# Second feed-forward matrix interleaved by tile and row half, both normalisations of a tile end to end, neighbour matrix split in two pieces among the roots

## The reference

```python
h1 = _layer_norm(x + attn_out, g1, be1)
ff = jax.nn.relu(h1 @ W1 + b1) @ W2 + b2
return _layer_norm(h1 + ff, g2, be2)          # added to x: "x1"
# next layer
h = jnp.maximum(_layernorm(x, axis=-1), 0.0)
alpha = x @ wc
beta = x @ wn                                  # x here is h
gamma = segment_sum(beta[dst], src) / counts[:, None]
x = x + alpha + gamma + bias
```

## Time and profile before

| what | us |
|---|---|
| median of 3 runs | 494.54 (494.07 to 494.81) |
| the profiled execution, as timed | 493.78 |
| its span in the profile | 491.9 |
| TensorE busy | 454.6 (92%) |
| VectorE busy | 309.4 (63%) |
| ScalarE busy | 192.4 (39%) |
| POOL busy | 164.3 (33%) |

### The profile page before, as it was taken

How to read it: one execution, slowest core, us unless ns; L and a number is a source line. 1 busy time by engine, 2 the same in 40 slices (tenths; PEclk the granted TensorE clock), 3 DMA queues, 4 the chain that set the end, 5 groups by cost and what they waited for, 6 DMA issues and landing times.

```text
span 491.9 us, 5957 instructions
## 1 busy us (share of the span) xinstructions
PE 454.6 (92%) x2107; PEld 333.7 (68%) x2107; DVE 309.4 (63%) x580; ACT 192.4 (39%) x265; POOL 164.3 (33%) x107
## 2 busy tenths in 40 slices
PE   3999997688869899889899999999999999999996
PEld 2456543334446778768678888888888888888865
DVE  5999845999975995877696223813361336142865
ACT  5878716546120531152351235222522342236240
POOL 3000141112242984539150433434342444145200
PEclk9999999999979999989998999999999999999999
DMA  8760000000030125202220023202321222220002
GB/s 267 205 225 1 1 1 23 0 1 0 1 107 0 52 94 198 85 1 107 88 83 4 0 98 139 95 12 87 120 88 71 87 107 85 87 85 1 0 1 85
DMA packets 22474, 34.34 MB, mean 70 GB/s; under 512 B 5680, under 2 KB 5936, under 8 KB 22448
## 3 DMA queue, kind: packets, MB, share of 16 engines
q1 hardware_dynamic: 22160, 33.85, 20.2%
q10 hardware_dynamic: 288, 0.13, 0.1%
HBM read 32.93 MB, written 1.05 MB: 69 GB/s over the span
## 4 chain that ended last, share of the span: by engine, by line
PE 70%; DVE 17%; POOL 5%; issue 3%; ACT 3%; DMA 1%; SPq 0%; POOLq 0%; DVEq 0%
PE ps L1177 15%; PE ps L1179 15%; PE ps L1178 15%; PE ps L1246 6%; PE ps L1239 4%; PE ps L1206 3%; PE ps L1205 3%; DVE rsum L894 3%; PE ps L1232 3%; DVE e_sb L375 2%; DVE stats L721 2%; POOL x_sb L479 1%; POOL w_lo L455 1%; DMA x_sb<-in_x 1%; DVE half_sum L891 1%
## 5 line engine op out<-in xcount | busy, mean ns | idle before, releaser
L454 POOL TENSOR_TENSOR w_lo<-w_stage,w_hi 128x1024 fp32r<-128x1024 f32 x22 | 52.7, 2394 | 137.7 <-ACT w_hi L530 137.7
L530 ACT ACTIVATE w_hi<-w_stage 128x2048 fp32r<-128x2048 f32 x23 | 44.0, 1911 | 73.0 <-PE ps L1179 73.0
L455 POOL TENSOR_TENSOR w_lo<-w_stage,w_hi 128x1024 fp32r<-128x1024 f32 x22 | 57.3, 2606 | 0.0
L1177 PE MATMUL ps<-w_hi,hid_hi 128*128 128x512 f32 x128 | 49.8, 389 | 0.0
L1178 PE MATMUL ps<-w_lo,hid_hi 128*128 128x512 f32 x128 | 49.8, 389 | 0.0
L1179 PE MATMUL ps<-w_hi,hid_lo 128*128 128x512 f32 x128 | 49.8, 389 | 0.0
L1086 DVE TENSOR_SCALAR tmp<-ps,bl 128x512 f32<-128x512 f32 x16 | 12.0, 751 | 52.1 <-ACT hid_hi L672 52.1
L1177 PE MATMUL ps<-T_hi,w_hi 128*128 128x512 f32 (+1 forms) x112 | 41.7, 372 | 1.8 <-DVE T_lo L751 1.4
L1178 PE MATMUL ps<-T_lo,w_hi 128*128 128x512 f32 (+1 forms) x112 | 40.7, 364 | 0.0
L1179 PE MATMUL ps<-T_hi,w_lo 128*128 128x512 f32 (+1 forms) x112 | 40.7, 363 | 0.0
L792 DVE TENSOR_SCALAR one_src<-iota_n,edge_m,edge_w 128x256 f16 x128 | 35.1, 399 | 0.0
(11 more groups left out here) (211 smaller groups left out, 1052.0 us busy)
## 6 DMA issues: line engine op xcount, KB each, us to landing
w_stage<-in_L_gnn_Wr SPq DMA_DIRECT2D x8, 1024.0 KB, 5.3
w_stage<-in_L_gnn_Wl SPq DMA_DIRECT2D x8, 1024.0 KB, 5.3
w_stage<-in_L_gnn_W SPq DMA_DIRECT2D x5, 1024.0 KB, 6.3
x_sb<-in_x SPq DMA_DIRECT2D x4, 256.0 KB, 3.7
w_q<-in_L_gnn_Wq SPq DMA_DIRECT2D x1, 1024.0 KB, 7.5
w_k<-in_L_gnn_Wk SPq DMA_DIRECT2D x1, 1024.0 KB, 10.0
w_v<-in_L_gnn_Wv SPq DMA_DIRECT2D x1, 1024.0 KB, 5.5
w_o<-in_L_gnn_Wo SPq DMA_DIRECT2D x1, 1024.0 KB, 8.9
```

The lines of the kernel that those rows point to most:

```text
L454: gp.tensor_tensor(w_lo[s][:, 0:2], stage[s][:, 0:2], f32(w_hi[s][:, 0:2]), ALU.subtract)
L455: gp.tensor_tensor(w_lo[s][:, 2:4], stage[s][:, 2:4], f32(w_hi[s][:, 2:4]), ALU.subtract)\
L530: nc.scalar.activation(w_hi[u % 2][:], stage[u % 2][:], ACT.Copy).then_inc(hi_made, 1)
L1177: nc.tensor.matmul(goal, a_hi, b_hi, start=start, stop=False, **kw)
```

## The change

Five lists of instructions are reordered; no computation is added or dropped. The diff without its shift of line numbers, cut where a part only repeats:

```diff
-    ln_order += [(LN2, 0)] + [x for t in range(1, NT) for x in ((LN2, t), (LN3, t - 1))] + [(LN3, NT - 1)]
+    ln_order += [(k, t) for t in range(NT) for k in (LN2, LN3)]
...
+            def split_lo_half(u, half):
+                if half == 0:
+                    gp.wait_ge(hi_made, u + 1)
+                s, k = u % 2, slice(2 * half, 2 * half + 2)
+                ins = gp.tensor_tensor(w_lo[s][:, k], stage[s][:, k], f32(w_hi[s][:, k]), ALU.subtract)
+                if half:
+                    ins.then_inc(lo_made, 1)
...
             split_lo(W2B)
-            split_lo(WN)
-            for k, t in ln_order[2 * NT:4 * NT]:
-                power(ln_no(k, t))
+            for t in range(2):
+                power(ln_no(LN2, t))
+                power(ln_no(LN3, t))
+            split_lo_half(WN, 0)
+            power(ln_no(LN2, 2))
+            split_lo_half(WN, 1)
+            power(ln_no(LN3, 2))
+            power(ln_no(LN2, 3))
+            power(ln_no(LN3, 3))
             split_lo(WC)
...
             split_hi(W2B)
+            normalise(LN3, 0, h_sb, x_sb, ACT.Relu)
             split_hi(WN)
+            normalise(LN3, 1, h_sb, x_sb, ACT.Relu)
+            transposed_hi(T3, 4, 0)
+            transposed_hi(T3, 4, 1)
+            normalise(LN3, 2, h_sb, x_sb, ACT.Relu)
             act.wait_ge(reach_done, 1)
...
-            for t in range(NT):
-                normalise(LN3, t, h_sb, x_sb, ACT.Relu)
-                transposed_hi(T3, 4, t)
-                if t == NT - 2:
-                    split_hi(WC)
+            transposed_hi(T3, 4, 2)
+            split_hi(WC)
+            normalise(LN3, 3, h_sb, x_sb, ACT.Relu)
+            transposed_hi(T3, 4, 3)
...
-            for t in range(NT):
+            def y_in(t):
...
-                if t >= 2:
-                    norm_shift(LN3, t - 2)
                 v.wait_ge(y2_read, t + 1)
                 norm_stats(LN2, t, h_sb)
-                if 1 <= t < NT - 1:
-                    x1_finish(t - 1)
+
+            for t in range(2):
+                y_in(t)
+                x1_finish(t)
+                norm_shift(LN3, t)
+            y_in(2)
+            x1_finish(2)
             transposed_lo(T3, 4, 0)
-            x1_finish(NT - 2)
+            norm_shift(LN3, 2)
+            y_in(3)
             transposed_lo(T3, 4, 1)
-            norm_shift(LN3, NT - 2)
-            x1_finish(NT - 1)
+            x1_finish(3)
             transposed_lo(T3, 4, 2)
-            norm_shift(LN3, NT - 1)
+            norm_shift(LN3, 3)
             transposed_lo(T3, 4, 3)
...
+            w2_rows(0, 0)
+            w2_rows(1, 0)
+            w2_rows(0, 1)
...
+            w2_rows(2, 0)
+            w2_rows(1, 1)
+            w2_rows(3, 0)
+            w2_rows(2, 1)
+            w2_rows(3, 1)
...
+            h1_rows(0)
+            h1_rows(1)
             pe.wait_ge(isd_split, 1)
...
             pe.wait_ge(deg_made, 1)
+            beta_rows(0)
+            h1_rows(2)
+            beta_rows(1)
+            h1_rows(3)
+            beta_rows(2)
+            beta_rows(3)
```

More of the change, by code:

```diff
@@ L1410, in _, with w2_rows @@
                 last.then_inc(ff_done, 1)
-            for half in range(2):
+            def w2_rows(t, half):
                 hi, lo = weights(W2A + half)
                 pe.wait_ge(ff_lo_made, DT * (half + 1))
[L1415 to L1429, removed]
-                    for t in range(NT):
-                        last = nc.tensor.matmul(ps[:, 4, col(t)], ones[:], tmp[:, t, 0:P], start=True, stop=True)
-                    last.then_inc(deg_done, 1)
+                for k in range(DT):
+                    f = half * DT + k
+                    last = mm3(ps[:, t, :], ff_hi[:, f, col(t)], ff_lo[:, f, col(t)], hi[:, k, :], lo[:, k, :],
+                               f == 0, f == FT - 1)
+                last.then_inc(w2_done if half else w2_half_done, 1)
@@ new lines, in _ @@
+            w2_rows(0, 0)
+            w2_rows(1, 0)
+            w2_rows(0, 1)
+            with pe.If(slow > 0):
+                for s in range(NT):
+                    count_transposes(ct_lo, 4 + s, s, c_lo_tr)
+                pe.wait_ge(c_lo_made, 1)
+            pe.wait_ge(diag_made, NT)
+            pe.wait_ge(ones_made, 1)
+            for t in range(NT):
+                last = nc.tensor.matmul(ps[:, 4, col(t)], ones[:], tmp[:, t, 0:P], start=True, stop=True)
+            last.then_inc(deg_done, 1)
@@ new lines, in _, with h1_rows, beta_rows @@
+            w2_rows(2, 0)
[3 more added lines that the diff above has]
+            w2_rows(3, 1)
+            def h1_rows(t):
+                if t == NT - 1:
+                    pe.wait_ge(reach_out, 1)
+                pe.wait_ge(ln_out, ln_out_no(LN3, t))
+                transposes(4 + t, t)
+            def beta_rows(t):
+                pe.wait_ge(tr_lo, split_no(T3, t))
+                pe.wait_ge(y2_read, t + 1)
+                rows_tile(t, t, weights(WN), beta_done)
@@ L1449, in _ @@
             pe.wait_ge(deg_made, 1)
-            w = weights(WN)
-            for t in range(NT):
-                if t == NT - 1:
-                    pe.wait_ge(reach_out, 1)
-                pe.wait_ge(ln_out, ln_out_no(LN3, t))
-                transposes(4 + t, t)
-                if t >= 1:
-                    pe.wait_ge(tr_lo, split_no(T3, t - 1))
-                    pe.wait_ge(y2_read, t)
-                    rows_tile(t - 1, t - 1, w, beta_done)
-            pe.wait_ge(tr_lo, split_no(T3, NT - 1))
-            pe.wait_ge(y2_read, NT)
-            rows_tile(NT - 1, NT - 1, w, beta_done)
+            beta_rows(0)
[4 more added lines that the diff above has]
+            beta_rows(3)
             w = weights(WC)
```

## The result

The changed kernel takes 500.62 us (median of 4 runs, 498.70 to 501.27) against 494.46 (4 runs, 494.07 to 494.81): ratio 1.0105, interval 1.0069 to 1.0141. It is slower, as forecast. The forecast of 498.0 was 2.6 us low and the median lies 0.6 us above the upper end of the range (500.0). Later comparisons ran the kernel before up to 25 times on a chip: 492.84 to 497.86, median 494.58.

The account below looks back on a forecast made before the run. It took TensorE, busy in 92% of the span, as the bound, so the change costs what it does to beta 0's start: 494.54 + 3.5 = 498.0 us. Range 493.6 to 500.0; likeliest case alone 496.7 to 500.0.

Parts of the forecast that it names:

- The measure: Edited stage: chain from beta 0 to last normalise stays 7.26 us, so the change costs what it does to beta 0's start.
- The TensorE part: Second feed-forward product: a new 1.2 us wait for W2B's low part; product ends at 206.3 against 205.0.
- The wait for W2B: TensorE before the third tile: 1.2 us waiting for W2B's low part, which it did not wait before.
- The VectorE part: y, LN2 and LN3 steps run end to end: 5.6 us a tile, with waits for POOL no longer hidden.
- The head start for tile 1: VectorE starts tile 1 at 199.1 instead of 199.78, the only head start in the new order.
- The POOL part: Two 2.4 us pieces of WN's low part hold VectorE's two-SBUF-input instructions; beta 0 at 214.6, +3.5 us.
- both starts: POOL's two WN pieces, behind powers VectorE awaits, start ahead of VectorE by 0.07 us; forecast chance 0.52.
- the two held instructions: Tile 1's shift and tile 2's second LN2 product: forecast about 2.3 and near 3 us, against 0.16 and 0.75.
- The rival in which VectorE wins both: VectorE starts ahead of both WN pieces; beta 0 at 211.35, +0.3, time 494.8, no change; chance 0.17.
- The rival in which nothing is held at all: VectorE's shift and product run beside POOL's pieces; beta 0 at 210.05, -1.0, time 492.7 to 493.5; chance 0.14.
- The clock: TensorE's granted clock: beta 0 taken at 4.26 us; a later dip near 262 may change by some 1.7 us.

Follow-up runs that it names:

- e11: The changed kernel with the gate's 48 small products scattered between the first expert's large products; 496.11 us, ratio 1.0032.
- e5: The changed kernel with a pause of one memset on POOL before the first piece of WN's low part and four before the second; 497.04 us, ratio 1.0027.
- e1: The changed kernel with a pause of one tiny memset on POOL before each piece of WN's low part; 499.45 us, ratio 1.0091.
- e2: The changed kernel with the one-column shift written as a tensor_scalar, with one SBUF tensor and a pointer scalar; 498.72 us, ratio 1.0084.
- e4: The kernel before, with the gate's 48 products in two lots of 24 behind the expert's first two column blocks; 495.70 us, ratio 1.0011.
- e7: The kernel before, with the gate's 48 products scattered in threes and sixes between the first expert's large products; 492.15 us, ratio 0.9938.
- e9: The kernel before, with the gate's products scattered and POOL waiting for LN4's last R_lo; 490.21 us, ratio 0.9911.
- e10: The changed kernel with the longer pauses of e5, the gate's products scattered and POOL waiting for LN4's last R_lo; 490.55 us, ratio 0.9925.
- e3: The kernel before, with the one-column shift written as a tensor_scalar, with one SBUF tensor and a pointer scalar; 495.36 us, ratio 1.0017.
- e6: The changed kernel with only TensorE's second feed-forward product put back to halves, degree product between; 503.10 us, ratio 1.0152.
- e8: The kernel before, with POOL waiting for LN4's last R_lo before making the low part of the first expert's second matrix; 494.42 us, ratio 0.9979.

## Why the prediction was right, and where it was short

The way and the mechanism came as forecast; of the 6.2 us by which the medians differ, the forecast had 3.5.

- **The measure.** "The change costs what it does to the start of beta 0" held: the chain from beta 0 to normalise 3 was 7.29 against 7.26 us, and from beta 0 to the end of alpha 25.07 against 25.01. The second agreement is partly luck: this stretch depends on how much of it falls in a half clock, and over all thirteen profiles it is 24.9 to 26.4 us (26.4 in e11, whose beta 0 starts at the same +32.16).
- **The TensorE part.** The wait for W2B, the degree product and the fourth first-half tile came as worked out: WN's high part starts at 201.91, 18.8 us after the product's start; the forecast had 18.8 (201.06 less 182.23).
- **The VectorE part.** 5.6 us for a tile: 199.90 - 194.28 = 5.62. The head start for tile 1 was 0.7 us by forecast (199.1 against 199.78), and is 199.90 - 0.87 = 199.03.
- **The POOL part.** POOL won both starts. The sum gave +3.5 us at beta 0; measured +3.30, of which e5 shows 3.16 to go with the two held instructions; e1 and e5 show that VectorE's instruction runs free when it starts 0.10 us or more ahead of the piece, and e2 that the shift with one tensor input isn't held. The rival in which VectorE wins both was worked out as +0.3, and e5, which makes it win, gave +0.14. The rival in which nothing is held at all is refuted by the rows.
- **The clock.** This is the term that was mis-sized. The forecast let a dip near 262 "become longer or shorter by some 1.7 us" around zero. It cost 3.23 us in the profile, and the row of gate products is worth 3.6 to 4.5 us between after and e11. The working put the dip down to no cause. The earlier trace rows would not have given it: there a half clock follows a stretch in which TensorE was nearly idle, while in the row of 48 products of 4 columns it is shown as busy all the time (5.20 of 5.20 us). Only the row itself, which stood in the trace of the kernel before, pointed at it.

All eight profiles with the products in one row have a half clock that begins 2.2 to 5.2 us behind the first of them, and e4 has one behind each lot; the four with the products scattered (e7, e9, e10, e11) have none from 255 to 486. How long it lasts goes with how much of the row was left when the clock fell: 10.2 us with 21 to 27 products to go (after, e1, e2), 6.8 with 12 to 17 (e3, e5, e6, e8), 3.4 with none (before). The profile before is thus the best case of its kind: e3, with the old order and 6.8 us at half clock, takes 39.91 us for the gate's part, so about half of the 3.23 us is the luck of that execution.

Whether the change itself makes the long dip likelier, or 4 executions (498.70 to 501.27) happened on it, is not settled. e5 and e6, which are the changed kernel with an edit each and have a late alpha too, had the shorter dip in their profiles. The mean granted clock of the whole execution says something: it was 0.971 or 0.972 in all four of the changed kernel; in the kernel before it was 0.971 to 0.985 from run to run, and in the comparison with e1 to e4 its three runs at 0.972 took 497.0 to 497.9 (one at 0.971 took 495.2), against a median of 494.6 over all 25. At an equal clock of 0.972 the two kernels differ by 3.6 us (501.2 against 497.6, from two comparisons), about what the edited stage costs. What sets where a dip falls was not tried.

## What to carry to other kernels

Before a GpSimd instruction over SBUF is moved, list the VectorE instructions with two SBUF tensors that can start while it runs. The worst place is directly behind a small GpSimd result that VectorE waits for: VectorE comes 0.06 to 0.14 us late and pays for the whole of it (2.0 to 2.2 us more here). Make GpSimd wait until VectorE is through (e8); taking one of the two tensors as a pointer scalar freed the shift of one column, but look at the trace afterwards, since L950 was held with one SBUF input. Freeing a single instruction may only pass the hold-up on to the next (e3).

A row of many tiny matmuls counts as busy in a profile and may still cost the clock. Spread them between large ones; here that gained 0.6%, where reordering the stage that the change was about gained nothing.
